# Three borders between the stages of a four-layer kernel: the next stage's weights loaded in the stage before, first tokens rounded straight from PSUM

## What is computed

```
x = x + tanh(g_xattn[0]) * L0_xattn(layernorm(x), ctx, ctx)     # 16 heads of 16, context of 77 vectors
x = x + tanh(g_ffn[0])   * L0_ffn(layernorm(x))                 # ternary weights, hidden 1024
x = x + tanh(g_xattn[1]) * L1_xattn(layernorm(x), ctx)          # 8 heads of 64, a second layer norm inside
x = x + tanh(g_ffn[1])   * L1_ffn(layernorm(x))                 # self-attention, 8 heads of 64
```

## Time and profile before

| | us |
|---|---|
| median of 3 runs | 1993.03 |
| lowest, highest | 1991.8, 1994.41 |
| profiled execution | 1992.12 |
| span of the profiled execution | 1990.4 |
| stage A (to 254.6) | 254.6 |
| stage F (254.6 to 944.7) | 690.1 |
| stage C (944.7 to 1210.2) | 265.5 |
| stage E (1210.2 to the end) | 780.2 |

### The profile page before, as it was taken

The page is one execution under the profiler, slowest core; times in us unless marked ns, Lnnn a source line. Parts: engine busy times, 40 slices in busy tenths (PEclk is TensorE's granted clock), DMA queues, the critical chain, the costliest instruction groups (busy, mean ns, idle before and its releaser), DMA issues. The chain is left out here.

```text
span 1990.4 us, 60604 instructions
## 1 busy us (share of the span) xinstructions
PE 1845.3 (93%) x26589; PEld 1496.7 (75%) x26589; DVE 1184.3 (60%) x1654; ACT 1085.9 (55%) x1900; POOL 728.7 (37%) x1012
## 2 busy tenths in 40 slices
PE   6898779999999999998799987899999999999997
PEld 4666568787887878887678776788777887887875
DVE  7787522332323233242555543888888898888885
ACT  4666433443434344342455543677777777767763
POOL 6878601000010000000333331556655665656552
PEclk9999989999999999999799998999999999999999
DMA  5331000000000000000301004322332243223211
GB/s 178 99 101 56 23 27 1 22 21 1 22 1 22 22 1 22 0 22 12 110 28 44 30 22 118 87 66 63 93 104 58 60 109 93 61 62 109 78 51 35
DMA packets 147004, 106.23 MB, mean 53 GB/s; under 512 B 19992, under 2 KB 143152, under 8 KB 146736
## 3 DMA queue, kind: packets, MB, share of 16 engines
q1 hardware_dynamic: 146736, 102.28, 17.4%
HBM read 76.77 MB, written 25.49 MB: 51 GB/s over the span
## 5 line engine op out<-in xcount | busy, mean ns | idle before, releaser
L2264 ACT ACTIVATE E_prob<-E_ps_s,E_negmax 128x1024 f32<-128x1024 f32 x256 | 284.9, 1115 | 144.2 <-DVE E_negmax L2577 143.7
L2577 DVE TENSOR_REDUCE E_negmax<-E_ps_s 128x1 f32<-128x1024 f32 x256 | 301.4, 1219 | 82.6 <-PE E_ps_s L2084 82.2
L2584 DVE STREAM_TRANSPOSE E_prob<-E_prob 128x1024 f32<-128x1024 f32 x256 | 303.9, 1225 | 24.0 <-ACT E_prob L2264 11.5
L2103 PEld LDWEIGHTS E_ps_o<-E_prob,E_vrep 32*64 32x64 f32 x15872 | 231.1, 130 | 64.5 <-ACT E_part L2290 56.7
L2103 PE MATMUL E_ps_o<-E_prob,E_vrep 32*64 32x128 f32 x15872 | 262.5, 274 | 13.4 <-issue 3.9
L1690 ACT ACTIVATE F_raw<-F_ps,ffn_scales 128x512 f32<-128x512 f32 x128 | 88.3, 690 | 288.0 <-PE F_ps L1599 288.0
L1599 PE MATMUL F_ps<-F_ha,ffn_w_rounded 128*128 128x512 f32 x1024 | 240.7, 395 | 0.0
L1599 PE MATMUL F_ps<-F_hb,ffn_w_rounded 128*128 128x512 f32 x1024 | 240.2, 395 | 0.0
L1599 PEld LDWEIGHTS F_ps<-F_ha,ffn_w_rounded 128*128 128x128 f32 x1024 | 190.9, 188 | 48.4 <-issue 1.7
L1599 PEld LDWEIGHTS F_ps<-F_hb,ffn_w_rounded 128*128 128x128 f32 x1024 | 192.0, 188 | 46.9
L2480 POOL TENSOR_TENSOR E_part<-E_part 128x512 f32<-128x512 f32 x93 | 119.4, 1284 | 249.6 <-ACT E_part L2290 249.6
(11 more groups left out here) (315 smaller groups left out, 3912.7 us busy)
## 6 DMA issues: line engine op xcount, KB each, us to landing
E_vrep<-E_v_all SPq DMA_DIRECT2D x128, 256.0 KB, 3.0
A_w_stage<-in_L_ffn_h_wT SPq DMA_DIRECT2D x16, 512.0 KB, 3.9
E_v_all<-E_vst SPq DMA_DIRECT2D x32, 256.0 KB, 2.2
C_x<-x SPq DMA_DIRECT2D x20, 256.0 KB, 6.7
F_x<-x SPq DMA_DIRECT2D x9, 512.0 KB, 3.7
A_x<-in_x SPq DMA_DIRECT2D x16, 256.0 KB, 5.5
x<-A_x SPq DMA_DIRECT2D x16, 256.0 KB, 2.2
x<-F_x SPq DMA_DIRECT2D x8, 512.0 KB, 2.9
```

The lines of the kernel that those rows point to most:

```text
L2103: mm = pe.matmul(low[64 * j:64 * j + 64, g, :], vrep[rows, slot, KB // 4 * (quarter % 2) + k, dh * j:dh * (j + 1)], prob[rows, u % 2, :, j ...
L2264: act.activation(prob[:, s // UT % 2, s % UT, j, :], ps_s[:, j, :], ACT.Exp, bias=negmax[:, at:at + 1], scale=1.0, accum_out=den[:, 2 * c ...
L2577: dve.tensor_reduce(negmax[:, at:at + 1], ps_s[:, j, :], AX.X, ALU.max, negate=True).then_inc(d_max, 1)
L2584: dve.transpose(at, at).then_inc(d_t, 1)
```

## The change

Five things are changed.

- **Loads for C.** Wq, Wk, Wv and Wo of C, the first context and the LayerNorm vectors are loaded by F's SP program, in its last block, behind the load of C's first x. The four weights go into `shared`, a buffer of four parts of 128x1024 that lives through the whole kernel and that A uses as its staging buffer `w_stage`. C's SP program starts with the x pairs.
- **Loads for E.** Wq, Wk of the first heads and Wv are loaded in C, behind the store of pair 12 of 0 to 15, into `e_w` and `e_raw` (before: `w_raw` and `raw`, at the start of E). In E, `xt` and `xb` now lie in `shared` and `part` in `head`.
- **Start of F.** ACT rounds the first block from PSUM in two halves, DVE takes the low parts from PSUM half by half. This block's copy into `xt` and POOL's difference are gone.
- **Start of E.** ACT rounds the four groups from PSUM, DVE takes all four low parts from PSUM, and ACT copies the groups to SBUF afterwards, each once DVE has read it. The first scores, whose PSUM banks the groups lie in, wait for these copies. ACT rounds Wv behind the first three k and q parts; POOL no longer has groups 0 and 2.
- **Stores of F.** Each block is stored in two halves, each once it is done.

```
-            load_w(2, wq_raw, wqT)
-            load_ctx(0)
-            load_w(0, wk, wkT)
...
-            load_w(1, wv, wvT)
             for n in range(PB):
                 load_x(n)
-            load_w(3, wo_raw, woT)
             load_ctx(1)
...
+                if n == NP - 4:
+                    for dst, src in later:
+                        sp.dma_start(dst, src).then_inc(s_later, 16)
+            sp.wait_ge(s_later, 16 * len(later))
...
-                    sp.wait_ge(x_out[1 - u], 16 * (i + u))
+                    sp.wait_ge(x_out[1 - u], 32 * (i + u))
                 sp.dma_start(x[:, 1 - u, :, :], xd[0] if last else xs[b + 1]).then_inc(x_in[1 - u], 16)
+                if last:
+                    for dst, src in early:
+                        sp.dma_start(dst, src).then_inc(s_early, 16)
+                sp.wait_ge(d_y, 2 * b + 1)
+                sp.dma_start(xd[b, :, 0:2, :], x[:, u, 0:2, :]).then_inc(x_out[u], 16)
                 sp.wait_ge(d_y, 2 * b + 2)
-                sp.dma_start(xd[b], x[:, u, :, :]).then_inc(x_out[u], 16)
+                sp.dma_start(xd[b, :, 2:4, :], x[:, u, 2:4, :]).then_inc(x_out[u], 16)
...
-            x_out_of_psum(0)
+            if exact:
+                act.wait_ge(e_xt, 1)
+                act.activation(xt_part[0][:, 0, :], ps_x[:, 0, :], ACT.Copy).then_inc(first_hi, 1)
+                act.activation(xt_part[0][:, 1, :], ps_x[:, 1, :], ACT.Copy).then_inc(xt_hi, 1)
+                act.sem_inc(xt_raw, 1)
+            else:
+                x_out_of_psum(0)
...
+            if exact:
+                for c in range(DC):
+                    dve.wait_ge(xt_hi if c else first_hi, 1)
+                    ins = dve.tensor_tensor(xt_part[1][:, c, :], ps_x[:, c, :], xt_part[0][:, c, :], ALU.subtract)
+                ins.then_inc(xt_lo, 1)
...
-                    pe.wait_ge(c_lo, n + 1)
-                    pe.wait_ge(c_lo0, n + 1)
+                    pe.wait_ge(c_lo0, 2 * n + 2)
                 qk_proj(kind, n, (banks[i],)).then_inc(done[kind], 1)
                 if i == 2:
+                    pe.wait_ge(free["x"], NQ)
                     scores(0, 0, True)
...
-            act.wait_ge(wv_in, 16)
-            act.activation(wv[0][:, :, :], wv_raw[:, :, :], ACT.Copy).then_inc(wv_hi, 1)
             for q in range(NQ):
                 act.wait_ge(done["x"], q + 1)
+                act.activation(xt_part[0][:, :, q * PAIR:(q + 1) * PAIR], banks[4 + q].rearrange("p (k w) -> p k w", k=DC),
+                               ACT.Copy).then_inc(c_hi, 1)
+            for q in range(NQ):
+                act.wait_ge(c_lo0, q + 1)
                 x_out(q, banks[4 + q].rearrange("p (i w) -> p i w", w=TOK)).then_inc(free["x"], 1)
-                convert(q, q)
             first_qk("k", 0, banks[0])
             first_qk("q", 0, banks[1])
             first_qk("k", 1, banks[2])
+            act.activation(wv[0][:, :, :], wv_raw[:, :, :], ACT.Copy).then_inc(wv_hi, 1)
...
-            for q in (1, 3):
+            for q in range(NQ):
                 dve.wait_ge(c_hi, q + 1)
                 cols = slice(q * PAIR, (q + 1) * PAIR)
-                dve.tensor_tensor(xt_part[1][:, :, cols], xt[:, :, cols], xt_part[0][:, :, cols],
-                                  ALU.subtract).then_inc(c_lo0, 1)
+                dve.tensor_tensor(xt_part[1][:, :, cols], banks[4 + q].rearrange("p (k w) -> p k w", k=DC),
+                                  xt_part[0][:, :, cols], ALU.subtract).then_inc(c_lo0, 1)
```

More of the change, by code:

```diff
@@ L98, in newton, with first_attention @@
         own.step(eng.tensor_tensor(y, y, t, ALU.mult))
[L101 removed]
+def first_attention(nc, ident, gates, gates_src, x_src, x_dst, ctxT, wqT, wkT, wvT, woT, bias, H, ffn, head, w_stage, tag):
     B, _, S = ctxT.shape
@@ L849, in _, with cross_attention @@
             dve.wait_ge(d_inexact, 1)
-def cross_attention(nc, ident, gate, x_src, x_dst, ctxT, wqT, wkT, wvT, woT, bias, ln2, H, head, ahead, tag, setup=None):
+def cross_attention(nc, ident, gate, x_src, x_dst, ctxT, wqT, wkT, wvT, woT, bias, ln2, H, head, early, ahead, later, tag, setup=None):
     B, _, S = ctxT.shape
@@ L1501, in chunk, with feed_forward @@
         return w[:, at + k * width + a:at + k * width + b]
-def feed_forward(nc, ident, gate, x_src, x_dst, fw, w, scales, s3, head, exact, tag):
+def feed_forward(nc, ident, gate, x_src, x_dst, fw, w, scales, s3, head, early, exact, tag):
     BT = 4
@@ L2725, in gated_layers @@
         head = ctx.enter_context(nc.sbuf_tensor("head", [P, 4, D], F32))
+        shared = ctx.enter_context(nc.sbuf_tensor("shared", [P, STAGE, WCH], F32))
+        c_ctx = ctx.enter_context(nc.sbuf_tensor("c_ctx", [P, 2, DC, t["ctxT"].shape[2]], F32))
+        c_ln = ctx.enter_context(nc.sbuf_tensor("c_ln", [P, 2, DC], F32))
+        HD, rows = t["L1_xattn_Wq"].shape[1], "(c p) n -> p c n"
+        c_wq, c_wk, c_wv = (shared[:, i, :].rearrange("p (c n) -> p c n", n=HD) for i in range(3))
+        c_wo = shared[:, 3, :].rearrange("p (c n) -> p c n", n=D)
+        early = ((c_wq, t["L1_xattn_Wq"].rearrange(rows, p=P)),
+                 (c_ln[:, 0, :], t["L1_xattn_ln_scale"]), (c_ln[:, 1, :], t["L1_xattn_ln_bias"]),
+                 (c_ctx[:, 0, :, :], t["ctxT"][0].rearrange(rows, p=P)),
+                 (c_wk, t["L1_xattn_Wk"].rearrange(rows, p=P)), (c_wv, t["L1_xattn_Wv"].rearrange(rows, p=P)),
+                 (c_wo, t["L1_xattn_Wo"].rearrange(rows, p=P)))
         with ExitStack() as ffn_ctx:
```

77 lines of the change are left out of this document (25 added, 52 removed).

## The result

The changed kernel takes **1977.86 us** (median of 7 runs, 1975.85 to 1984.6). The kernel before takes 1991.8 in 7 runs beside it (1988.04 to 1994.41). The ratio is 0.9936, with a 95% interval from 0.9921 to 0.9951. On two other chips the same comparison gave 0.994 (0.9919 to 0.9961) and 0.993 (0.991 to 0.995). So the change is worth 12 to 14 us, where the sum said 16.1. The forecast of 1976.9 was closer to the time than the sum was to the gain, because the three runs it started from had a median 1.2 us above that of the seven.

A forecast was written before the change was run, and what follows sets the result against it. PE is busy for 93% of the span, so gains were sought at stage borders where it has nothing to do: 2.6 + 0.8 + 4.8 + 7.9 = 16.1 us, 1993.0 - 16.1 = 1976.9 us, range 1974.0 to 1981.0.

The forecast's parts named there:

- F's start: Border A to F: rounding from PSUM in halves starts PE's first product at 258.9 instead of 261.53, gain 2.6 us.
- C's start: Start of C: with loads already there, PE goes on at 949.0 instead of 953.79, so q_proj comes 4.8 us earlier.
- q_proj's own time: In C: q_proj, mostly at half clock, kept at 4.65 us, with a range of -1.8 and +1.1.
- rival 3: C: PE's 3.1 us come from instructions fetched beside big loads and shrink, or clock favours q_proj; up to 3 less; chance 0.10.
- PE's 3.1 us after C's first row: Start of C: PE's transposes begin 3.1 us after POOL's first row, for no reason that the profile shows.
- E's start: Start of E: products 6.2 us earlier, a further 1.7 from full clock; first scores 7.9 earlier in all.
- Rival 1: Clock gives nothing in E, products still 6.1 us, and q_proj has no full-clock part; 1978.6 to 1979.7; chance 0.20.
- Rival 2: ACT isn't ready at E's start, so products come 2.2 us later; 1979.1; chance 0.10.
- The tie at Wv: In E: POOL's Wv difference done at 1222.5, PE asks at 1222.6; won by 0.5 if POOL takes nearer 2.34.
- Lengths within 1 us each: F, C and E behind the border points keep their lengths within 1 us; E longer by over 5 makes the sum wrong.
- Rival 5: New buffer places slow E's slot: at 100 ns more per exponential (1115 ns before), 2002.5; chance 0.03.
- Rival 4: C doesn't pass its lead on, x tiles or third pair's normalisation being last: all 4.8 lost, 1981.7; chance 0.07.

The follow-up runs named there:

- shift_4k: Changed kernel with 32 transposes (64 PE instructions) added in the branch that is never executed; profiled span 1984.0 us.
- after_beside: The changed kernel once more, unedited, run beside the kernels with shifted instructions; 1977.91 us (6 runs), ratio 0.993 to the kernel before.
- bo_first: Changed kernel with the output bias's rounding (ACT) and difference (DVE) moved ahead of Wv's; 1978.91 us against 1979.28 for the changed kernel on the same chip.

## Why the prediction was right, and where not

- **F's start, 2.6.** Measured 2.62, and 4.05 to 4.07 in all twelve profiles with the new start. The two roundings took 0.60 and DVE's two differences 1.29, close to the rows of E that stood in for them.
- **F's stores, 0.8.** Measured 0.80 from the last issue to C's first row, with 256 KB landing in 2.1.
- **C's start, 4.8.** Measured 4.94 from C's first row to q_proj (10.93 us; 10.70 to 11.08 in the other profiles with the same start of C, shift_4k apart). The bias, Wq and DVE's rounded Wq (ready at 948.3) were all in time, as worked out.
- **q_proj's own time, kept at 4.65.** It came out shorter in this execution. Here are two stretches of the kernel before, then two of the changed one, each from about the start of q_proj (granted clock third from the end):

```profile
960.00:962.00 2.00, 2.00 (x11) 2.00 (x11) 1.59 (x5) 0.61 (x4) 1.26 (x7) 0.50 1.09 350
962.00:964.00 2.00, 2.00 (x12) 2.00 (x11) 0.01 (x1) 0.00 (x0) 1.48 (x7) 0.50 0.73 233
```

```profile
950.00:952.00 2.00, 2.00 (x10) 2.00 (x10) 1.90 (x14) 0.42 (x4) 0.00 (x0) 0.50 1.07 345
952.00:954.00 2.00, 2.00 (x15) 2.00 (x15) 1.60 (x7) 0.20 (x2) 1.12 (x6) 0.79 0.53 168
```

  The clock rises 1.6 us into q_proj now, where it rose only 3.4 us into it, so it takes 3.85, and the first scores come 5.47 behind its start instead of 6.28. This is not a fixed gain: the changed kernel's other two profiles have 3.87 and 4.92 for it. In all, C from q_proj on is 1.7 shorter here, and 0 to 2 among the executions of the table. That is inside the stated 1.8, on the side that rival 3 had named for its second half.
- **PE's 3.1 us after C's first row, "for no reason that the profile shows".** It is a wait for instructions, as the first half of rival 3 had it, but the big loads have no part in it that shows. PE's first transpose follows the end of a moved 16 KB piece of instructions by 1.35 to 1.42 us in all fourteen profiles. In the kernel before the piece is moved from 945.38 to 946.51, now from 940.96 to 942.23. With the big loads gone from C's start the stretch came out as 3.3 here and as 3.1 to 3.5 in the other profiles with early loads: it doesn't shrink.
- **E's start, 7.9.** Measured 7.73: products 6.07 earlier (6.2), clock 1.7 (1.7). Rival 1 falls by the granted clock, by products of 0.39 us and by the kernel in which PE was made to stand. The Trainium skill's sentence in "TensorE: Matmul & The Clock Gate", section "Part 4: PE-mode transpose", that the full clock doesn't engage for transposes, doesn't hold here: it went from 0.50 to 1.00 in a stretch with hardly anything else (0.75 in 1201 to 1203, with transposes until 1202.48). Rival 2 falls too, as ACT began at 1199.15, with PE. A risk stayed: in after_beside and bo_first the clock rose later, the first product still took 0.77, and the start 9.6.
- **The tie at Wv, won by 0.5.** POOL's difference took 2.40 and the first v product began 0.5 after its end. But the reason given, that DVE's new differences read PSUM, overlooked an operation that reads two SBUF operands: the bias's, which the new order had pushed into POOL's 2.4 us. Here the failing step is that only the moved and new instructions were put beside POOL's, and not those that a moved instruction pushes along. The section "Who interferes with whom" of the Trainium skill's "SBUF — State Buffer" covers it: two SBUF inputs on DVE and a read on POOL, and whoever is first holds the other off. The rows agree, 0.42 against 2.42. Price: 1.2 at slot 0, 0.6 from slot 1 on.
- **"Lengths within 1 us each".** True for F, false for C behind q_proj (1.7 shorter) and for E: 767.7 behind the scores instead of 763.1. The text said that over 5 would make the sum wrong; 4.6 is short of that, and the sum came out 16.1 against 14.3 in the profiles and 12 to 14 in the times. Of the 4.6, 0.6 is the bias and 2.2 are PE's longer waits for instructions in the slots; the remaining 1.8 are not accounted for. One profile of each kernel can't tell such a difference from chance: the same stretch varies from 729 to 739 among kernels with nearly the same work. The bound of 1 us had no row behind it. Rival 5, slower by buffer places, falls: the exponential takes 1114 ns (1115 in the earlier trace rows).
- **Rival 4**, C not passing its lead on: falls, C passed on all it got and 1.7 more.

The mechanisms at the three borders held to 0.2 us each, and their sum did: 16.1. The total did not, by 2 to 4 us. That the time fell so near the forecast is in part luck. In the profiled execution a surplus in A (1.1) and C (1.7), which the prediction had not claimed, made up for more than half of the loss in E (4.6); the borders and E's loss alone give 11.5 us, and 1993.0 - 11.5 = 1981.5 lies just outside the range. The three runs that the forecast started from, 1.2 us high, did the rest.

## What to carry to other kernels

A border is best costed from PE's own first row in the stage to its first large product: such a stretch repeated to some hundredths where no load and no late instruction fell into it, while a long loop of the same instructions varies by several us, and a gain of 10 us can be followed in a timeline and hardly in the time. Before loads are moved into an earlier stage, put those of the stage in the order in which they are needed: that alone gave 3.1 of the 4.9 us here, or 2.0 of 3.8 by the other execution of the old start. When an instruction is moved, look at what it pushes along: a difference of 8x256 that nobody thought of held up the first row maximum by 1.2 us, since DVE read two SBUF operands while POOL did.

## What was not expected of the hardware

- Instructions that are never executed changed the places where PE stands, by up to 3 us at a place (C's start in shift_4k, slot 100 there). With 128 of them the ratio to the kernel before was 0.9961 instead of 0.993 to 0.994; that this is their cost is not shown.
- PE's stands without a visible wait in E, 135 of 0.5 us or more in fourteen profiles, all end 1.2 to 1.6 us after a 16 KB piece of instructions has been moved, and so does its standing ahead of C's first transposes (1.35 to 1.42).
- The granted clock rose to 1.00 under 16 fp32 transposes, and was lost again when PE then stood for 3.67 us, with the fall some 0.7 us ahead of the first product: it cost 2.84 us up to the first scores, more than the 1.7 worked out.
- An operation with 8 partitions and 256 elements took 2.42 us instead of 0.42, from 1208.89 to 1211.31, while POOL's of 128x1024 ran from 1208.63 to 1211.03.
